# Key sums on VectorE: the second half of a key block is subtracted one step later, and the sums of the batch before are turned and read ahead of the key block

## The chip, the cores and the metric

One core of a Trainium2 chip runs the whole program in one launch. The metric is the device time of the program in microseconds (us), median over several runs; lower is better.

## What is computed

The reference is a small decoder layer stack over x (8 batches of 56 tokens, 256 wide) and a context of 8 batches of 1500 tokens: softmax cross attention, a mixture of experts, a linear cross attention, a second mixture of experts, each with a residual. The change touches only what the linear cross attention takes from the context:

```python
# linear cross attention (L1), per batch and head (16 heads of 16, 64 features)
k = (ctx @ Wk.T + bk)                      # 1500 x 256
v = (ctx @ Wv.T + bv)                      # 1500 x 256
k_prime = relu(einsum('bhnd,fd->bhnf', k, Wkf)) * mask
kv    = einsum('bhnf,bhne->bhfe', k_prime, v)   # 64 x 16 per head
k_sum = sum(k_prime, axis=2)                    # 64 per head
```

All matrix products keep about float32 accuracy: each operand x is held as a rounded part (hi, type fp32r) and a rest (lo = x - hi), and a product is three matmuls: lo by hi, hi by lo, hi by hi (`mm3`, L102 to L106).

## The kernel before

The program has two stages. The first, `sums_and_queries` (L109), computes kv and k_sum of all eight batches, and beside it the normalised queries of the softmax attention. It ends in a barrier of all engines, then `attention_and_after` runs the rest. The change is in the first stage alone.

**Steps.** A batch of 1500 context tokens is 12 steps t of 125 tokens (`KT`), and 3 chunks of 500 (`KC`), 4 steps to a chunk. `step(i, first, last)` is written once for each engine and holds all 12 steps of batch i; `run_peeled` (L217) runs batch 0 by itself (`first`), batches 1 to 6 in a hardware loop, and batch 7 by itself (`last`). Engines meet only through semaphores, and each works through its own list in order.

**A step on TensorE** (L372): `values(i, t)` (6 matmuls into one of two PSUM banks `vals_ps`), `features(i, t)` (8 matmuls in two halves of 4, L282), at every third step `add`, which accumulates vs by kp of three earlier steps into `sums` (L296), then what `keys_at` gives for this step, then the turn of the batch before at t == 4, and for two heads of queries a batch `project` (t = 4 and 8) and `mean_square` (t = 6 and 10, L344).

**Key blocks.** `keys_at` (L208) gives, outside the last batch, one key block at t = 0, 2, 4, 6, 8 and 10: block (c, m) is 500 tokens of chunk c by 128 of the 256 key columns, one chunk ahead of the steps that use it. `keys` on TensorE (L264) makes it in the single bank `keys_ps`, 6 matmuls, after a wait until VectorE has taken both halves of the block before (`ks_lo`, L266). Then come two halves h of 64 partitions each: ScalarE writes the rounded part plus bias (L421, `ks_hi`), VectorE writes the rest (L537, `ks_lo`), which reads `keys_ps`, the bias and ScalarE's result in partitions 0 to 63, and writes partitions 64 to 127 of `ks`. In the last batch the blocks are at t = 0, 2, 3 and 5.

**VectorE's step** (L599): L605 takes values out of PSUM into vs (after `v_done`), L609 takes the second half of the features into kp with relu (after `feat_done`, gives `kp_high`); ScalarE takes the first half (L474, gives `kp_low`). Each half of `feat` is a single bank, so each half of `features(i, t + 1)` waits for `kp_low` or `kp_high` of step t (L288):

```python
for half in range(2):
    wait(pe, ks_lo, 4 * (i * KC + c) + 2 * (half + 1))
    wait(pe, (kp_low, kp_high)[half], i * KT + t)
```

Behind L609 VectorE runs both halves of a key block (L611), at t == 4 `read_blocks` of the batch before (L541), then `round_square` of a query head (L559, at t = 5 and 9) and `normalise` (L565, at t = 7 and 11). `round_square` feeds `split_square` on POOL (L687), and that `mean_square` on TensorE one step later.

**Turn and read.** At t == 3 ScalarE copies the finished sums of the batch before to SBUF (`take_sums`, four L428, `kv_taken`). At t == 4 TensorE transposes them (`turn`, L315, two transposes into the second half of the `sums` bank pair, L319), and VectorE reads the result in six instructions (L548, L550, L554, `kv_done`). `add(i, 0)`, at t == 5, waits for `kv_done` (L304), since it starts `sums` anew.

Of the kernel before, what the change touches and what calls it, by code (L numbers as in the profile page):

```python
# [60 lines left out]
def wait(eng, sem, value):  # L61

    if isinstance(value, int) and value <= 0:
        return
    eng.wait_ge(sem, value)
# [43 lines left out]
def sums_and_queries(nc, kv, qT, q0, raw, ct, kk, wk0, wv0, a, ident):  # L109
# [9 lines left out]
    with ExitStack() as ctx:  # L119
# [84 lines left out]
        def queries_at(i, last, t, after):  # L204

            return [(n, 2 * i + n) for n in range(2) if t - after == ((0, 3) if last else (4, 8))[n]]

        def keys_at(i, last, t):  # L208

            c, n = divmod(t, TPC)  # L210
            if last:
                return {0: [(i, 1, 0)], 2: [(i, 1, 1)], 3: [(i, 2, 0)], 5: [(i, 2, 1)]}.get(t, [])
            if n not in (0, 2):
                return []
            return [(i, c + 1, n // 2)] if c + 1 < KC else [(i + 1, 0, n // 2)]
# [47 lines left out]
        def _(pe):  # L263
# [9 lines left out]
            def values(i, t):  # L273
                c, n = divmod(t, TPC)
                y = slice(n * KP, (n + 1) * KP)
                wait(pe, v_set, i * KT + t - 1)
                for k in range(DC):
                    last = mm3(nc, vals_ps[0:KP, t % 2, 0:D], ct[0][:, c, k, y], ct[1][:, c, k, y],
                               wv[0][:, k, :], wv[1][:, k, :], k == 0, k == DC - 1)
                last.then_inc(v_done, 1)  # L280
# [15 lines left out]
            def add(i, g):  # L296

                n = i * KT + (g + 1) * GROUP
                wait(pe, v_set, n)
                wait(pe, v_mask, n)  # L300
                wait(pe, kp_low, n)
                wait(pe, kp_high, n)
                if g == 0:
                    wait(pe, kv_done, 4 * i)  # L304
                for t in range(g * GROUP, (g + 1) * GROUP):
                    for r in range(4):
                        for j in range(4):
                            h = 8 * (r // 2) + 2 * j + r % 2
                            last = nc.tensor.matmul(sums[32 * j:32 * j + RV, 0, r * FD:(r + 1) * FD],
                                                    vs[:, t % RING, h, :], kp[:, t % RING, h * FD:(h + 1) * FD],  # L310
                                                    start=(t == 0 and r == 0), stop=(t == KT - 1 and r == 3),
                                                    skip_group_check=True)
                last.then_inc(sums_done, 1)

            def turn(i):  # L315

                wait(pe, kv_taken, 4 * (i + 1))
                for n in range(2):
                    last = nc.tensor.transpose(sums[:, 1, n * 128:(n + 1) * 128], sums_sb[:, n * 128:(n + 1) * 128],  # L319
                                               ident[:])  # L320
                last.then_inc(kv_turned, 1)
# [50 lines left out]
            def step(i, first, last):  # L372
                for t in range(KT):
                    values(i, t)
                    features(i, t)
                    if t % GROUP == GROUP - 1:
                        if t >= GROUP:
                            add(i, t // GROUP - 1)
                        elif not first:
                            add(i - 1, NG - 1)  # L380
                    for which in keys_at(i, last, t):
                        keys(*which)
                    if t == 4 and not first:
                        turn(i - 1)
                    if last and t > FIRST_KEYS_AT:
                        key_mean(t - FIRST_KEYS_AT - 1)
                    if last and t >= FIRST_KEYS_AT:
                        key_project(t - FIRST_KEYS_AT)
                    for k, h in queries_at(i, last, t, MEAN_AT):
                        mean_square(h, k)  # L390
                    for k, h in queries_at(i, last, t, 0):
                        project(h, k, i)
# [136 lines left out]

        @block.vector  # L530
        def _(dve):
            def keys(i, c, m):

                for h in range(2):
                    y = slice(64 * h, 64 * (h + 1))
                    wait(dve, ks_hi, 4 * (i * KC + c) + 2 * m + h + 1)
                    nc.vector.scalar_tensor_tensor(ks[64:128, c, 2 * m + h, :], keys_ps[y, 0:CH],  # L537
                                                   bk[y, m:m + 1], ks[0:64, c, 2 * m + h, :].bitcast(F32),
                                                   ALU.add, ALU.subtract).then_inc(ks_lo, 1)

            def read_blocks(i):  # L541

                wait(dve, kv_turned, i + 1)
                src = sums[:, 1, :].rearrange("p (h n) -> p h n", n=32)
                to = kv[:, one(context(i))].rearrange("p a h n -> p (a h) n")
                for n in range(2):
                    r = slice(64 * n, 64 * (n + 1))
                    nc.vector.tensor_tensor(tmp[r], bv[r, :, n, :], src[r, :, HE:RV].to_broadcast([64, NP, HE]),  # L548
                                            ALU.mult).then_inc(tmp_done, 1)
                    nc.vector.tensor_copy(to[r, :, HE], src[r, :, HE]).then_inc(kv_done, 1)  # L550
                for n in range(2):
                    r = slice(64 * n, 64 * (n + 1))
                    wait(dve, tmp_done, 2 * i + n + 1)
                    nc.vector.tensor_tensor(to[r, :, 0:HE], tmp[r], src[r, :, 0:HE], ALU.add).then_inc(kv_done, 1)  # L554
# [44 lines left out]
            def step(i, first, last):  # L599
                for t in range(KT):  # L600
                    m = i * KT + t
                    if t % GROUP == 0:
                        wait(dve, sums_done, NG * i + t // GROUP - 1)
                    wait(dve, v_done, m + 1)
                    nc.vector.tensor_scalar(vs[:, t % RING, :, 0:HE],  # L605
                                            vals_ps[0:KP, t % 2, 0:D].rearrange("p (h e) -> p h e", e=HE),
                                            masks[:, one(context(i) * KT + t), 0], None, ALU.mult).then_inc(v_set, 1)
                    wait(dve, feat_done, 2 * m + 2)
                    nc.vector.tensor_scalar(kp[:, t % RING, 512:1024], feat[0:KP, 1, :], 0.0, None,  # L609
                                            ALU.max).then_inc(kp_high, 1)  # L610
                    for which in keys_at(i, last, t):  # L611
                        keys(*which)
                    if t == 4 and not first:
                        read_blocks(i - 1)
                    if last and t > FIRST_KEYS_AT:
                        key_normalise(t - FIRST_KEYS_AT - 1)
                    if last and t in (7, 8):
                        split_first_queries(t - 7)
                    for k, h in queries_at(i, last, t, SQUARE_AT):
                        round_square(h, k)  # L620
                    for k, h in queries_at(i, last, t, ROOT_AT[last]):
                        normalise(h, k)
                    if first and t == 5:
                        dve.wait_ge(nw_loaded, 32)
                        nc.vector.scalar_tensor_tensor(nw[:, 2:3], nw[:, 0:1], HD ** -0.5, nw[:, 1:2],
                                                       ALU.mult, ALU.mult).then_inc(nw_done, 1)
                        dve.wait_ge(nw_done, 1)
# [27 lines left out]
                                    ALU.subtract).then_inc(f_split, 1)  # L655
            dve.wait_ge(const_loaded, 32)
            dve.wait_ge(set0, 5)
            keys(0, 0, 0)
            for c in range(DC):
                dve.wait_ge(x_hi, c + 1)  # L660
                nc.vector.tensor_tensor(xnT[1][:, c, :], (proj, mean)[c][:, 0:NTOK], xnT[0][:, c, :].bitcast(F32),
                                        ALU.subtract).then_inc((proj_free, mean_free)[c], 1)
            keys(0, 0, 1)
            dve.wait_ge(m_loaded, 16)
            run_peeled(dve, step)
            key_normalise(NK - 1)
# [90 lines left out]
class Norm:  # L757
# [81 lines left out]
    def turn(self, pe, h):  # L839

        pe.wait_ge(self.xn_done, 2 * h + 2)
        for c in range(DC):
            for i in range(2):
                y = c * HT + i * TP
                last = self.nc.tensor.transpose(self.bank[:, 6, y:y + TP],
                                                self.scratch[:, 2 * h + i, c * 128:(c + 1) * 128], self.ident[0:TP, 0:TP])
        last.then_inc(self.turned_done, 1)
# [1627 lines left out]
```

## Time and profile before

| | |
|---|---|
| median of three runs | 1281.7 us (1280.79 to 1281.98) |
| the profiled execution | 1282.82 us |
| its span, first to last instruction | 1281.0 us, so 1.8 us lie around it |
| TensorE busy in the span | 1186.6 us (93%) |
| VectorE, ScalarE, POOL busy | 876.8, 737.7, 536.0 us |
| mean granted TensorE clock | 0.982 of full speed |

Engines in the profile: PE is TensorE's matmuls, PEld its weight loads (one before each matmul), DVE is VectorE, ACT ScalarE, POOL GpSimd, SP SyncE. L12 is line 12 of the kernel. A row of the timeline has start and length in us, engine, line, operation, the tile written and the tiles read, shapes, the count of instructions merged into the row, and in brackets the idle time before it with what ended it. The first stage fills the span up to about 372 us; its loop batches repeat each other to within some hundredths of a microsecond.

### The profile page before, as it was taken

The page shows a single profiled execution, that of the slowest core. Times are in us where ns is not written, and L with a number is a line of the kernel's source. Part 1 is how long each engine was busy: PE and PEld are TensorE (multiplying, and loading weights), DVE is VectorE, ACT ScalarE, POOL GpSimd, SP SyncE. Part 2 cuts the span into 40 slices and gives each one's busy share as a digit, 9 for nine tenths or more (in the row PEclk, how much of TensorE's full clock was granted, in tenths as well). Part 3 has the DMA queues.
Part 4 walks back from the last instruction along what each step waited for, and adds up shares of the span by engine and source line. Part 5 has one row for each costly group of instructions (what it writes and reads, how often), then busy time and mean ns, then how long its engine had stood idle before and what let it go on. Part 6 is the DMA issues. An engine that isn't in the chain of part 4 may idle for free.

```text
span 1281.0 us, 28260 instructions
## 1 busy us (share of the span) xinstructions
PE 1186.6 (93%) x10014; PEld 1055.1 (82%) x10014; DVE 876.8 (68%) x1950; ACT 737.7 (58%) x1330; POOL 536.0 (42%) x561
## 2 busy tenths in 40 slices
PE   5999999999877999999999999999999996898988
PEld 4888888888756878888888788887888896887888
DVE  5656665666556887878878887878787653656664
ACT  4655655655545656667576666665666643545432
POOL 2423232323135365363553544636536674633400
PEclk9999999999988999999999999999999998999999
DMA  4211111110013101111011110110001025014000
GB/s 142 75 43 41 56 32 40 56 40 1 2 40 106 49 25 35 39 48 48 1 47 48 45 51 0 48 48 20 28 0 50 18 75 161 2 52 123 1 8 9
DMA packets 42689, 56.12 MB, mean 44 GB/s; under 512 B 3410, under 2 KB 41602, under 8 KB 42626
## 3 DMA queue, kind: packets, MB, share of 16 engines
q1 hardware_dynamic: 41810, 54.23, 13.4%
q10 hardware_dynamic: 816, 1.05, 0.3%
q8 instruction: 40, 0.66, 0.2%
q14 instruction: 23, 0.19, 0.0%
HBM read 54.81 MB, written 0.46 MB: 43 GB/s over the span
## 4 chain that ended last, share of the span: by engine, by line
PE 57%; DVE 7%; DMA 2%; issue 2%; ACT 2%; SPq 1%; POOL 1%; DVEq 0%; ACTq 0%
PE att_bank L104 16%; PE att_bank L106 14%; PE att_bank L105 14%; PE att_bank L1854 6%; PE att_bank L1812 3%; DMA att_raw_n<-in_ctx 1%; DVE att_cn L2109 1%; DVE att_pr L2163 1%; DMA tail_x<-in_x 1%; SPq L1290 1%; DVE tail_full L1428 1%; PE att_bank L1566 1%; DVE tail_hid L1447 0%; PE att_bank L939 0%; PE att_bank L1384 0%
## 5 line engine op out<-in xcount | busy, mean ns | idle before, releaser
L2335 POOL TENSOR_TENSOR att_sq<-att_work,att_sq 128x500 fp32r<-128x500 f32 x90 | 119.8, 1331 | 160.1 <-DVE att_sq L2129 160.1
L2339 POOL TENSOR_TENSOR attention_kk<-att_work,attention_kk 128x500 fp32r<-128x500 f32 x90 | 121.9, 1354 | 154.1 <-DVE attention_kk L2137 154.1
L104 PE MATMUL att_bank<-att_pT,att_cn 125*128 125x448 f32 x384 | 157.0, 409 | 7.3 <-DVE att_pT L2178 6.6
L1992 ACT ACTIVATE att_pr<-att_pr,att_nmx 112x1500 f32<-112x1500 f32 (+1 forms) x96 | 108.5, 1130 | 71.0 <-DVE att_nmx L2166 71.0
L106 PE MATMUL att_bank<-att_pT,att_cn 125*128 125x448 f32 x384 | 140.9, 367 | 0.0
L105 PE MATMUL att_bank<-att_pT,att_cn 125*128 125x448 f32 x384 | 140.4, 366 | 0.0
L537 DVE SCALAR_TENSOR_TENSOR attention_kk<-kvs_keys_ps,kvs_bk,attention_kk 64x500 fp32r<-64x500 f32 x96 | 70.9, 738 | 92.0 <-ACT attention_kk L421 90.4
L2178 DVE TENSOR_TENSOR att_pT<-att_bank,att_pT 125x448 fp32r<-125x448 f32 x192 | 118.3, 617 | 14.6 <-ACT att_pT L2008 14.3
L2163 DVE TENSOR_SCALAR_CACHE_REDUCE att_pr<-att_bank 112x500 f32<-112x500 f32 x192 | 121.7, 675 | 5.9 <-PE att_bank L106 4.5
L292 PE MATMUL kvs_feat<-kvs_f,attention_kk 128*125 128x256 f32 x768 | 113.0, 284 | 10.8 <-DVE kvs_kp L609 10.1
L1854 PEld LDWEIGHTS att_bank<-all_ident,att_pr 112*125 112x125 f32 x768 | 109.6, 189 | 14.4 <-ACT att_pr L1992 2.3
L421 ACT ACTIVATE attention_kk<-kvs_keys_ps,kvs_bk 64x500 fp32r<-64x500 f32 x96 | 64.7, 674 | 92.6 <-PE kvs_keys_ps L106 91.3
L1854 PE MATMUL att_bank<-all_ident,att_pr 112*125 112x112 f32 x768 | 111.2, 271 | 1.7 <-ACT att_pr L1992 1.7
L292 PEld LDWEIGHTS kvs_feat<-kvs_f,attention_kk 128*125 128x125 f32 x768 | 98.6, 186 | 15.9 <-issue 14.1
L1981 ACT ACTIVATE att_work<-att_bank,att_eps 128x500 f32<-128x500 f32 x90 | 60.7, 674 | 86.8 <-PE att_bank L106 86.8
L2008 ACT ACTIVATE att_pT<-att_bank 125x448 fp32r<-125x448 f32 x192 | 102.2, 532 | 11.4 <-PE att_bank L1854 11.4
L2132 DVE TENSOR_TENSOR att_work<-att_bank,att_work 128x500 f32<-128x500 f32 x90 | 60.9, 677 | 56.4 <-ACT att_work L1988 55.8
L104 PE MATMUL att_bank<-attention_kk,attention_q 128*112 128x500 f32 x192 | 77.4, 403 | 16.6 <-DVE att_pr L2163 11.3
L474 ACT ACTIVATE kvs_kp<-kvs_feat,kvs_zero 125x512 f32<-125x512 f32 x96 | 65.8, 686 | 43.1 <-PE kvs_feat L292 42.6
L1986 ACT ACTIVATE att_work<-att_bank,att_eps 128x500 f32<-128x500 f32 x90 | 61.0, 677 | 48.2 <-PE att_bank L1812 48.2
L104 PEld LDWEIGHTS att_bank<-att_pT,att_cn 125*128 125x128 f32 x384 | 73.2, 191 | 17.5 <-DVE att_pT L2178 11.7
L2129 DVE CAST att_sq<-att_work 128x500 fp32r<-128x500 f32 x90 | 51.4, 571 | 40.1 <-ACT att_work L1981 40.1
(279 smaller groups left out, 3416.9 us busy)
## 6 DMA issues: line engine op xcount, KB each, us to landing
attention_raw_t<-in_ctxT SPq DMA_DIRECT2D x45, 500.0 KB, 4.0
att_raw_n<-in_ctx SPq DMA_DIRECT2D x16, 750.0 KB
kvs_raw_q<-in_wq SPq DMA_DIRECT2D x8, 256.0 KB, 3.9
tail_wo_raw<-in_wo SPq DMA_DIRECT2D x4, 512.0 KB, 4.4
tail_down_w<-in_down SPq DMA_DIRECT2D x8, 256.0 KB, 3.8
tail_gate_w<-in_gate SPq DMA_DIRECT2D x7, 256.0 KB, 2.8
tail_up_w<-in_up SPq DMA_DIRECT2D x7, 256.0 KB, 3.1
tail_gate_w<-in_gate SPq DMA_DIRECT2D x1, 1760.0 KB, 7.0
```

What stands on the lines that cost most here:

```text
L104: nc.tensor.matmul(out, w_lo, x_hi, start=start, stop=False, skip_group_check=True)
L105: nc.tensor.matmul(out, w_hi, x_lo, start=False, stop=False, skip_group_check=True)
L106: return nc.tensor.matmul(out, w_hi, x_hi, start=False, stop=stop, skip_group_check=True)
L292: last = nc.tensor.matmul(feat[0:KP, half, z], ks[:, c, 2 * half + g, y], f2[:, w, :], start=(w == 1), stop=(w == 0), skip_group_check=True)
L537: nc.vector.scalar_tensor_tensor(ks[64:128, c, 2 * m + h, :], keys_ps[y, 0:CH], bk[y, m:m + 1], ks[0:64, c, 2 * m + h, :].bitcast(F32), AL ...
L1854: last = nc.tensor.transpose(ring[0:KP, t % 3, j * TP:(j + 1) * TP], pr[:, j, t * KP:(t + 1) * KP], ident[0:TP, 0:TP])
L1992: nc.scalar.activation(pr[:, j, keys], pr[:, j, keys], ACT.Exp, scale=-1.0, bias=nmx[:, j:j + 1], accum_out=z[:, 4 * u + j, c:c + 1]).then ...
L2008: nc.scalar.activation(pT[0][:, t % 3, :], ring[0:KP, t % 3, 0:QU], ACT.Copy).then_inc(pT_hi, 1)
L2163: nc.vector.tensor_scalar(pr[:, j, c * CH:(c + 1) * CH], ring[0:TP, c, 0:CH], -1.0, 3.0e38, ALU.mult, ALU.min, accum_out=mn[:, j, c:c + 1] ...
L2178: nc.vector.tensor_tensor(pT[1][:, t % 3, :], ring[0:KP, t % 3, 0:QU], pT[0][:, t % 3, :].bitcast(F32), ALU.subtract).then_inc(ring_free, 1)
L2335: nc.gpsimd.tensor_tensor(sq[1][:, i % 2, :], work[:, i % 2, :], sq[0][:, i % 2, :].bitcast(F32), ALU.subtract).then_inc(sq_lo, 1)
L2339: nc.gpsimd.tensor_tensor(kk[:, c, 2 + gi, :], work[:, i % 2, :], kk[:, c, gi, :].bitcast(F32), ALU.subtract).then_inc(k_lo, 1)
```

## The change

TensorE does the turn of the batch before ahead of the key block of t == 4 and no longer behind it. VectorE reads the turned sums ahead of that block. Outside the last batch VectorE subtracts only the first half of a key block in the block's own step; the second half comes in the next step, behind that step's L605 and L609 and ahead of `round_square` and `normalise`. Blocks are only at even t up to 10, so none is left over at a batch's end. The last batch and the two blocks ahead of batch 0 keep both halves together. No instruction is added or taken away, on any engine or DMA queue.

```diff
@@ TensorE, step
+                    if t == 4 and not first:
+                        turn(i - 1)
                     for which in keys_at(i, last, t):
                         keys(*which)
-                    if t == 4 and not first:
-                        turn(i - 1)
@@ VectorE
-            def keys(i, c, m):
-
-                for h in range(2):
+            def keys(i, c, m, halves):
+
+                for h in halves:
                     y = slice(64 * h, 64 * (h + 1))
                     wait(dve, ks_hi, 4 * (i * KC + c) + 2 * m + h + 1)
@@ VectorE, step
                     wait(dve, feat_done, 2 * m + 2)
                     nc.vector.tensor_scalar(kp[:, t % RING, 512:1024], feat[0:KP, 1, :], 0.0, None,
                                             ALU.max).then_inc(kp_high, 1)
-                    for which in keys_at(i, last, t):
-                        keys(*which)
                     if t == 4 and not first:
                         read_blocks(i - 1)
+                    if not last and t > 0:
+                        for which in keys_at(i, last, t - 1):
+                            keys(*which, (1,))
+                    for which in keys_at(i, last, t):
+                        keys(*which, (0, 1) if last else (0,))
@@ VectorE, ahead of batch 0
-            keys(0, 0, 0)
+            keys(0, 0, 0, (0, 1))
...
-            keys(0, 0, 1)
+            keys(0, 0, 1, (0, 1))
```

## Rows read from the trace of the kernel before

**Rows 1.** Busy time by stretch, us; then granted clock, DMA share, GB/s
```profile
core 0: us, PE busy (x) PEld busy (x) DVE busy (x) ACT busy (x) POOL busy (x), PEclk, DMA share, GB/s
102.00:144.00 42.00, 39.60 (x648) 36.16 (x638) 25.77 (x48) 24.46 (x40) 12.73 (x18) 1.00 0.15 43
...
372.00:392.00 20.00, 14.69 (x60) 11.12 (x60) 10.62 (x41) 10.92 (x18) 5.82 (x12) 0.84 0.53 141
```

**Rows 2.** Waits of PE, 30 to 370 us: total, times, longest
```profile
PE kvs_feat L292 <- DVE kvs_kp L609: 9.6, 20, 0.6
PE kvs_sums L309 <- DVE all_kv L554: 5.6, 7, 0.8
```

**Rows 3.** Timeline of weight loads, a loop batch, t = 4 to project
```profile
115.77 0.53 PEld L292 LDWEIGHTS kvs_feat<-kvs_f,attention_kk 128*125 128x125 f32 x4
117.08 0.54 PEld L292 LDWEIGHTS kvs_feat<-kvs_f,attention_kk 128*125 128x125 f32 x4 [0.77 <-issue]
117.55 0.19 PEld L104 LDWEIGHTS kvs_keys_ps<-attention_ct,kvs_wk 128*128 128x128 f32 x1
...
118.79 0.36 PEld L319 LDWEIGHTS kvs_sums<-all_ident,kvs_sums_sb 128*128 128x128 f32 x2
119.12 0.19 PEld L104 LDWEIGHTS kvs_proj<-kvs_xnT,kvs_wq 128*128 128x128 f32 x1
```

**Rows 4.** Timeline of VectorE, the same loop batch, t = 2 to 5
```profile
114.34 1.51 DVE L537 SCALAR_TENSOR_TENSOR attention_kk<-kvs_keys_ps,kvs_bk,attention_kk 64x500 fp32r<-64x500 f32 x2 [3.05 <-ACT attention_kk L421]
115.88 0.48 DVE L605 TENSOR_SCALAR kvs_vs<-kvs_vals_ps,kvs_masks 125x256 f32<-125x256 f32 x1
116.28 0.68 DVE L609 TENSOR_SCALAR kvs_kp<-kvs_feat 125x512 f32<-125x512 f32 x1
116.88 0.48 DVE L605 TENSOR_SCALAR kvs_vs<-kvs_vals_ps,kvs_masks 125x256 f32<-125x256 f32 x1
...
121.54 0.28 DVE L548 TENSOR_TENSOR kvs_tmp<-kvs_bv,kvs_sums 64x128 f32<-64x128 f32 x1
121.75 0.16 DVE L550 COPY all_kv<-kvs_sums 64x8 f32 x1
121.94 0.29 DVE L548 TENSOR_TENSOR kvs_tmp<-kvs_bv,kvs_sums 64x128 f32<-64x128 f32 x1
...
122.98 0.48 DVE L605 TENSOR_SCALAR kvs_vs<-kvs_vals_ps,kvs_masks 125x256 f32<-125x256 f32 x1
```

**Rows 5.** Timeline of weight loads: batch 0, then t = 5, 8 and 11
```profile
29.50 0.53 PEld L292 LDWEIGHTS kvs_feat<-kvs_f,attention_kk 128*125 128x125 f32 x4 [0.71 <-issue]
...
121.05 1.01 PEld L292 LDWEIGHTS kvs_feat<-kvs_f,attention_kk 128*125 128x125 f32 x8
...
123.07 1.39 PEld L309 LDWEIGHTS kvs_sums<-kvs_kp,kvs_vs 125*17 125x17 f32 x96 [1.00 <-issue]
...
130.32 0.54 PEld L292 LDWEIGHTS kvs_feat<-kvs_f,attention_kk 128*125 128x125 f32 x4
131.31 0.53 PEld L292 LDWEIGHTS kvs_feat<-kvs_f,attention_kk 128*125 128x125 f32 x4 [0.45 <-issue]
...
141.81 1.02 PEld L292 LDWEIGHTS kvs_feat<-kvs_f,attention_kk 128*125 128x125 f32 x8
142.97 1.36 PEld L309 LDWEIGHTS kvs_sums<-kvs_kp,kvs_vs 125*17 125x17 f32 x96
```

**Rows 6.** Timeline of ScalarE at t = 3: the four copies of take_sums
```profile
115.61 1.55 ACT L428 ACTIVATE kvs_sums_sb<-kvs_sums 17x256 f32<-17x256 f32 x4
```

**Rows 7.** Timeline of VectorE at t = 9
```profile
138.00 0.69 DVE L609 TENSOR_SCALAR kvs_kp<-kvs_feat 125x512 f32<-125x512 f32 x1 [0.16 <-PE kvs_feat L292]
138.76 0.39 DVE L559 CAST kvs_sq<-kvs_work 128x448 fp32r<-128x448 f32 x1
```

**Rows 8.** Timeline of POOL, t = 9
```profile
139.24 1.16 POOL L687 TENSOR_TENSOR kvs_sq<-kvs_work,kvs_sq 128x448 fp32r<-128x448 f32 x1 [5.29 <-DVE kvs_sq L559]
```

**Rows 9.** Timeline of weight loads, t = 10: key block and mean square
```profile
139.34 0.19 PEld L104 LDWEIGHTS kvs_keys_ps<-attention_ct,kvs_wk 128*128 128x128 f32 x1
...
140.59 0.41 PEld L349 LDWEIGHTS kvs_mean<-kvs_sq,kvs_mean_mat 128*128 128x128 f32 x2
```

## The prediction

> **What bounds the kernel now.** I read the busy times by stretch first. In a loop batch of the first stage TensorE's matmuls are busy for 39.60 of 42 us while VectorE has 25.77, ScalarE 24.46 and POOL 12.73, and the clock is granted in full [rows 1]. So TensorE sets the pace, and the stage gets shorter only by what TensorE stands still. Next I read who TensorE waits for in this stage. Two waits carry nearly all of it: the second half of the features waits for VectorE's L609, 20 times, and the sums wait for the read of the turned sums, 7 times [rows 2]. The change aims at these two. The stage ends in a barrier of all engines and the next one starts its own loads behind it, so I count a microsecond saved here as a microsecond of the total.
>
> The totals of the waits are too small, since a matmul's modelled end reaches into the gap, so I take sizes from the weight loads. At t = 4 the two halves of the features start at 115.77 and 117.08, and an unhindered half takes 117.55 - 117.08 = 0.47. The second could have started at 116.24: TensorE loses 0.84 [rows 3]. The cause is in VectorE's rows: two L537 of the key block from 114.34, L605 at 115.88, L609 at 116.28 to 116.96, and TensorE starts 0.12 after that end, which I use below as the lag from any engine to TensorE [rows 3, 4]. The same happens at t = 2 (no row shown, same sizes). At t = 8 the loss is 131.31 - (130.32 + 0.47) = 0.52 [rows 5]. At t = 5 the add starts at 123.07, where its features started at 121.05; undisturbed it comes 142.97 - 141.81 = 1.16 after them, so 0.86 is lost [rows 5]. Key blocks at t = 4, 8 and 10 lose nothing to their own second half: an add, a project or a mean square lies between the block and the features in question.
>
> **Part 1: the second half one step later.** One L537 with its gap is 0.77 (two take 115.88 - 114.34 = 1.54) [rows 4]. L605 and L609 of the step behind the block come 0.77 sooner: at t = 3, L609 at 115.51, done 116.19, TensorE served at 116.31. Against 116.24 that leaves 0.07, so **0.77 is gained at t = 4 and the same at t = 2**. At t = 8, 0.77 covers the whole 0.52: **0.52 gained**.
>
> What becomes late instead? The deferred L537 starts behind L609. How soon, the trace doesn't show for this pair, so I bound it: 0.60 after L609's start if it overlaps like the L605 at 116.88, or 0.03 after L609's end, 0.71, if it behaves like instructions that change their partition half [rows 4]. The two L548 and the L550 between them decide for me: L550, in the same half as the L548 ahead, starts 0.21 after that 0.28 long one, before it ends; the second L548, in the other half, starts 0.19 after a 0.16 long L550, behind its end [rows 4]. L537 writes the upper half, L609 the lower, so I take 0.71. The Trainium skill says the same against this change in "VectorE: DVE Perf Modes", section "Two Vector instructions with no wait between them": an instruction whose start quadrant differs from the last one's starts only when all earlier ones are done. By that rule the sum below stands, and the trace agrees as far as these rows go. With 0.60 instead of 0.71, the key block of t = 10 in seven batches and the two waits in batch 0 below would each be 0.11 shorter, a gain of 1 us more.
>
> So at t = 3 the deferred L537 runs 116.22 to 116.96 and TensorE knows at 117.08. Three waits hang on it:
> - The next key block needs `keys_ps` back. At t = 2 and 8 of a loop batch an add comes first, at t = 6 and 0 too (one step before): nothing; at t = 4 the turn (part 2) waits longer anyway. In batch 0 there is no add at t = 2 and no turn: the block can start at 29.50, where the stalled half starts now, and not 29.97; instead of 0.77 **0.47 is gained, twice** [rows 3, 5].
> - At t = 10 no add comes between. L609 of t = 9 starts at 138.00 because TensorE's features end there, so it doesn't move sooner. The deferred L537 runs 138.71 to 139.45, TensorE may start the block at 139.57 and not 139.34: **0.23 lost** [rows 7, 9].
> - L559 stands behind it: 139.48 for 138.76, 0.72 later. POOL's split follows, 139.96 for 139.24, done 141.12, and the mean square is served at 141.24. It would have been due at 140.59 + 0.23 = 140.82: **0.42 lost** [rows 7, 8, 9]. At t = 5 the same delay has more than 3 us before the mean square of t = 6, and I cost it at nothing. L565 at t = 7 and 11 waits for ScalarE anyway.
>
> **Part 2: turn and read first.** The turn needs ScalarE's four copies, done at 117.16 [rows 6]. That was covered by the key block. Now TensorE is through with the features at 116.31 + 0.47 = 116.78 and waits until 117.28. The turn costs the same 119.12 - 118.79 = 0.33 as before, the key block 118.79 - 117.55 = 1.24, so the project starts at 118.85 for 119.12. Of the 0.77 won at t = 4 **only 0.27 is left** [rows 3, 6]. If the lag from ScalarE is nothing, 0.39 is left.
> In return the read, 122.98 - 121.54 = 1.44 long, starts behind L609 of t = 4 at about 118.0 and ends by 119.5, where VectorE now stands idle waiting for ScalarE's half of the block, and `kv_done` is there well over 2 us before the add: **0.86 gained** [rows 4, 5]. If something unseen holds VectorE in that gap, the price is that the read goes behind again, and the 0.86 stays lost.
>
> **The sum.** Loop batch: 0.77 + 0.27 + 0.86 + 0.52 - 0.23 - 0.42 = 1.77, six times 10.6. Batch 0: 0.47 + 0.47 + 0.52 - 0.65 = 0.8. Batch 7: both halves stay together and no block stands at t = 4: 0. Together 11.4 us. From the profiled execution's 1282.8 that gives 1271.4; the median lies 1.1 lower, so 1270.3. The lags are rather rounded up, so I say **1270.0**.
>
> **Rivals.**
> - *A, both new waits stay away.* If the split is in time at t = 10 and the copies at t = 4, a loop batch gains 0.77 + 0.77 + 0.86 + 0.52 = 2.92 and batch 0 gains 2.06: 19.6 us, 1262.1. For it: the new waits are sums of several small lags. Against: the 0.50 at the turn follows from one row, and ScalarE's order isn't touched. If only the t = 10 losses stay away, it is 16 us, 1265.7. Chance of the two 0.18.
> - *B, the half isn't what TensorE waits for.* If `kp_low` of ScalarE were as late as `kp_high`, L609 would be served earlier for nothing: six times 0.86 is left, less seven times 0.65: 0.6 us, 1281.1. Against: the first half of the features, served by ScalarE, starts 1.31 before the second [rows 3]. Chance 0.03.
> - *C, slower: the deferred half holds up every block.* The mechanism is that of t = 10: the L537 now waits in line for an L609 that itself waits for TensorE, then TensorE waits for the L537 and for the square's split. If the 0.65 arose at all six blocks of seven batches, 27 us, less the 19.6 gained, the time would be 1289. It decides from a loss of 0.47 a block. Against: an add, the turn or a project stands ahead of or behind the other blocks, and only two blocks have a square behind them. Chance 0.02.
> - *D, the clock.* The lower level, 1.2 for 2.4 GHz, showed as 0.84 granted behind the barrier, where TensorE had stood still [rows 1]. The change makes the stage denser, and there the clock was full. A low stretch of 24 us would eat the gain and leave about 1281.7. Chance 0.02.
>
> **How the numbers follow.** My forecast has 0.75, with 8 to 15 us gained from the bounds above (stalls that come back in part, lags of 0 to 0.12). The range takes in the lesser form of A and ends ahead of B: 1264.5 to 1274.5. A measurement of this kernel can tell 0.2%, 2.6 us, from no change. Faster has the forecast and A, 0.93; within 0.2% B and D, 0.05; slower C, 0.02.
>
> **What would show it.** In a loop batch the 0.77 and 0.45 idle ahead of L292 (t = 2, 4, 8) and the 1.00 ahead of L309 (t = 5) should be gone; L319 should stand ahead of the key block with about 0.5 idle ended by ScalarE's L428; a short idle ahead of the key block of t = 10, and one of about 0.4 ahead of L349, ended by POOL. The batch's period should fall by 1.8 us, and the second stage keep its length. I am wrong if the period falls by under 1.2 or over 2.4, or if the second stage changes by over 2 us.

## The result and the profile after

The changed kernel takes 1274.87 us (median of five, 1273.24 to 1277.79) against 1281.83 us before (five runs beside it); the ratio is 0.9947, 95% interval 0.9933 to 0.9961. It is faster, by 7.0 us, where 11.7 were forecast, and 0.4 us beyond the range's upper end. The profiled execution took 1277.79 us, span 1276.0 us.

The gain came from where it was looked for, but not all of it. The second stage's first matmul starts at 366.47 us in the profile after, and at 373.29 before: the first stage is 6.8 us shorter, nearly the whole gain of the medians. The stretch of a loop batch, the same columns as in [rows 1]:

```profile
102.00:144.00 42.00, 41.04 (x621) 37.36 (x620) 26.65 (x48) 24.68 (x40) 14.03 (x20) 1.00 0.17 53
```

TensorE is busy for 41.04 of 42 us and not 39.60. What it still waits for between 20 and 370 us (total, times, longest), against [rows 2], whose window begins 10 us later:

```profile
PE kvs_feat L292 <- DVE attention_kk L537: 6.2, 15, 0.5
...
PE kvs_sums L309 <- DVE all_kv L554: 0.6, 1, 0.6
```

The wait for the read of the sums is gone but for the last batch. The features no longer wait for L609. They wait for **L537**, the very instruction that was moved, 15 times: twice in each of the seven batches outside the last, and once at the first step of batch 0. That last one isn't new. The kernel before has it too, at a time that the window of [rows 2] leaves out:

```profile
23.91 0.54 PEld L292 LDWEIGHTS kvs_feat<-kvs_f,attention_kk 128*125 128x125 f32 x4 [0.85 <-DVE attention_kk L537]
```

The weight loads say where; this is the loop batch that answers to [rows 3, 5, 9]:

```profile
113.67 0.53 PEld L292 LDWEIGHTS kvs_feat<-kvs_f,attention_kk 128*125 128x125 f32 x4
114.91 0.53 PEld L292 LDWEIGHTS kvs_feat<-kvs_f,attention_kk 128*125 128x125 f32 x4 [0.71 <-DVE attention_kk L537]
115.39 0.25 PEld L319 LDWEIGHTS kvs_sums<-all_ident,kvs_sums_sb 128*128 128x128 f32 x2
115.61 0.19 PEld L104 LDWEIGHTS kvs_keys_ps<-attention_ct,kvs_wk 128*128 128x128 f32 x1
...
118.87 1.02 PEld L292 LDWEIGHTS kvs_feat<-kvs_f,attention_kk 128*125 128x125 f32 x8
120.03 1.36 PEld L309 LDWEIGHTS kvs_sums<-kvs_kp,kvs_vs 125*17 125x17 f32 x96
...
127.27 0.54 PEld L292 LDWEIGHTS kvs_feat<-kvs_f,attention_kk 128*125 128x125 f32 x4
128.40 0.53 PEld L292 LDWEIGHTS kvs_feat<-kvs_f,attention_kk 128*125 128x125 f32 x4 [0.59 <-DVE attention_kk L537]
...
135.48 1.01 PEld L292 LDWEIGHTS kvs_feat<-kvs_f,attention_kk 128*125 128x125 f32 x8
136.61 0.19 PEld L104 LDWEIGHTS kvs_keys_ps<-attention_ct,kvs_wk 128*128 128x128 f32 x1
...
138.26 0.30 PEld L349 LDWEIGHTS kvs_mean<-kvs_sq,kvs_mean_mat 128*128 128x128 f32 x2 [0.44 <-POOL kvs_sq L690]
```

At t = 4 the second half of the features starts 114.91 - 113.67 = 1.24 after the first, where 0.47 is its own pace: 0.77 is lost, for 0.84 before. At t = 8 it is 128.40 - 127.27 - 0.47 = 0.66, for 0.52 before: more, not less. The add of t = 5 comes 1.16 after its features, undisturbed. At t = 10 the key block stands 1.13 behind the start of its features instead of the 0.94 or 0.95 of eight loads, and the mean square waits for POOL. At t = 2 no row has an idle time: that stall is gone.

VectorE's rows for t = 2 to 4, against [rows 4]:

```profile
112.24 0.73 DVE L537 SCALAR_TENSOR_TENSOR attention_kk<-kvs_keys_ps,kvs_bk,attention_kk 64x500 fp32r<-64x500 f32 x1 [2.73 <-ACT attention_kk L421]
113.00 0.48 DVE L605 TENSOR_SCALAR kvs_vs<-kvs_vals_ps,kvs_masks 125x256 f32<-125x256 f32 x1
113.40 0.68 DVE L609 TENSOR_SCALAR kvs_kp<-kvs_feat 125x512 f32<-125x512 f32 x1
114.11 0.75 DVE L537 SCALAR_TENSOR_TENSOR attention_kk<-kvs_keys_ps,kvs_bk,attention_kk 64x500 fp32r<-64x500 f32 x1
...
116.31 0.27 DVE L548 TENSOR_TENSOR kvs_tmp<-kvs_bv,kvs_sums 64x128 f32<-64x128 f32 x1
...
118.05 0.73 DVE L537 SCALAR_TENSOR_TENSOR attention_kk<-kvs_keys_ps,kvs_bk,attention_kk 64x500 fp32r<-64x500 f32 x1 [0.35 <-ACT attention_kk L421]
```

L609 did come sooner: done at 114.08, in time for TensorE's half, which was due at 113.67 + 0.47 = 114.14. The deferred L537 starts at 114.11, ends at 114.86, and TensorE goes on at 114.91. The code says why. Step 4 is the first step of chunk 1, and the second half of `features` waits at L287 for all four halves of that chunk's keys. The last of them is the second half of the block of t = 2: the half that was moved. The same holds for t = 8 and the block of t = 6. The deferral took L537 from ahead of L609 and put it behind, while both are wanted at the same instant.

My theory after reading this: of the deferral only the block of t = 0 pays; those of t = 2 and 6 bring nothing, that of t = 8 costs at t = 10. The rival is the prediction's account, in which t = 4 and 8 profit too. In all of what follows "batch" is the distance between the same load in two loop batches that follow each other: 41.60 us before (the stall of t = 2 stands at 109.82 and 151.41, which is 41.59), 155.34 - 114.91 = 40.43 after. Over the five distances from the stall of t = 4 in batch 1 to that in batch 6 the means are 41.61 and 40.47, and in every kernel below such a mean lies within 0.05 of the one distance given. So differences of a few hundredths between batches mean nothing.

### The profile page after: what moved, and what is told of

It is laid out like the page before. It is cut to its first block, busy times and chain, and to the rows that moved or that the text cites. A ratio compares the mean times of both kernels' runs of the same rounds, so it can differ in the third digit from the quotient of the medians.

```text
span 1276.0 us, 28260 instructions
## 1 busy us (share of the span) xinstructions
PE 1190.6 (93%) x10014; PEld 1056.9 (83%) x10014; DVE 879.2 (69%) x1950; ACT 738.2 (58%) x1330; POOL 536.0 (42%) x561
## 4 chain that ended last, share of the span: by engine, by line
PE 57%; DVE 7%; DMA 2%; issue 2%; ACT 2%; SPq 1%; POOL 1%; DVEq 0%; ACTq 0%
PE att_bank L104 16%; PE att_bank L106 14%; PE att_bank L105 14%; PE att_bank L1857 6%; PE att_bank L1815 3%; DMA att_raw_n<-in_ctx 1%; DVE att_cn L2112 1%; DVE att_pr L2166 1%; DMA tail_x<-in_x 1%; SPq L1293 1%; DVE tail_full L1431 1%; PE att_bank L1569 1%; DVE tail_hid L1450 0%; PE att_bank L942 0%; PE att_bank L1387 0%
## 5 line engine op out<-in xcount | busy, mean ns | idle before, releaser
L537 DVE SCALAR_TENSOR_TENSOR attention_kk<-kvs_keys_ps,kvs_bk,attention_kk 64x500 fp32r<-64x500 f32 x96 | 70.9, 738 | 81.5 <-ACT attention_kk L421 79.9
L104 PEld LDWEIGHTS att_bank<-att_pT,att_cn 125*128 125x128 f32 x384 | 73.2, 191 | 17.4 <-DVE att_pT L2181 11.7
```

The source lines that it names most:

```text
L104: nc.tensor.matmul(out, w_lo, x_hi, start=start, stop=False, skip_group_check=True)
```

## The experiments

### The turn and read alone

```diff
 # on the kernel before: the two moves around turn() and read_blocks(), and no deferral
+                    if t == 4 and not first:
+                        read_blocks(i - 1)
                     for which in keys_at(i, last, t):
                         keys(*which)
-                    if t == 4 and not first:
-                        read_blocks(i - 1)
```

> Only the turn and the read of the last batch's sums go ahead of the key block; both halves of a key block stay together. Theory (each stall of TensorE belongs to one named wait, and they add up): the 1.00 idle ahead of L309 at t = 5 goes, worth 0.86, and the turn costs 0.22 ahead of the block instead of 0.33 behind it; the stalls at t = 2, 4 and 8 (0.84, 0.84, 0.52) stay. A loop batch falls from 41.60 to about 40.65 us, the first stage by 5.7 us, the time to about 1276. Rival (the read was only late because the whole key block was): the read now ends earlier but the add still stands behind something else, and the batch stays above 41.2.

Measured: 1276.38 us, ratio 0.9952 (0.9935 to 0.9969). Weight loads of one loop batch, and the first stall of the next:

```profile
108.77 0.52 PEld L292 LDWEIGHTS kvs_feat<-kvs_f,attention_kk 128*125 128x125 f32 x4 [0.78 <-issue]
115.99 0.53 PEld L292 LDWEIGHTS kvs_feat<-kvs_f,attention_kk 128*125 128x125 f32 x4 [0.77 <-issue]
129.34 0.53 PEld L292 LDWEIGHTS kvs_feat<-kvs_f,attention_kk 128*125 128x125 f32 x4 [0.45 <-issue]
...
149.44 0.53 PEld L292 LDWEIGHTS kvs_feat<-kvs_f,attention_kk 128*125 128x125 f32 x4 [0.79 <-issue]
```

The three stalls of the features stand as before, the one of the add is gone, and the batch is 40.67 us. This part alone brings 0.93 a batch, most of what the whole change brings.

### The deferral alone

```diff
 # on the changed kernel: TensorE's turn behind the key block again, and VectorE's read behind it
-                    if t == 4 and not first:
-                        read_blocks(i - 1)
                     if not last and t > 0:
...
                         keys(*which, (0, 1) if last else (0,))
+                    if t == 4 and not first:
+                        read_blocks(i - 1)
```

> Only the second half of a key block is deferred; the turn stays behind the key block and the read behind the block's first half. Theory (the features of a chunk's first step need that chunk's own second key block complete, L287): 0.77 gained at t = 2, 0.07 at t = 4 and 0.14 lost at t = 8, both then waiting for L537, about 0.54 lost at t = 10; the read of t = 4 starts one L537 sooner, so that the add of t = 5 loses almost nothing: 0.8 gained. Batch about 40.65 us, time about 1276. Rival (the recorded prediction: deferral gives 0.77, 0.77 and 0.52 and loses 0.65): 1.4 from these plus the 0.8 of the read, batch 39.4 us.

Measured: 1276.57 us, ratio 0.9957 (0.9941 to 0.9974).

```profile
115.42 0.53 PEld L292 LDWEIGHTS kvs_feat<-kvs_f,attention_kk 128*125 128x125 f32 x4 [0.72 <-DVE attention_kk L537]
120.63 1.39 PEld L309 LDWEIGHTS kvs_sums<-kvs_kp,kvs_vs 125*17 125x17 f32 x96 [0.23 <-issue]
129.03 0.53 PEld L292 LDWEIGHTS kvs_feat<-kvs_f,attention_kk 128*125 128x125 f32 x4 [0.59 <-DVE attention_kk L537]
...
156.04 0.53 PEld L292 LDWEIGHTS kvs_feat<-kvs_f,attention_kk 128*125 128x125 f32 x4 [0.71 <-DVE attention_kk L537]
```

The batch is 40.62 us, where the rival wanted 39.4, and both stalls are ended by L537. The two parts are not independent: with one L537 fewer ahead of the read, the add's idle time falls from 1.00 to 0.23 although the turn wasn't moved. So the parts alone bring 0.93 and 0.98, and both at once 1.17 and not 1.91: the stall of the add is counted in both.

### Deferring the block of t = 0 only

```diff
-                    if not last and t > 0:
+                    if not last and t - 1 in (0,):
...
-                        keys(*which, (0, 1) if last else (0,))
+                        keys(*which, (0,) if not last and t in (0,) else (0, 1))
```

> Turn and read ahead as in the changed kernel, but only the block of t = 0 is deferred; those of t = 2, 4, 6, 8 and 10 keep both halves together. Theory: 0.77 at t = 2, 0.86 at t = 5, 0.11 at the turn, nothing lost at t = 8 and 10, the stall of t = 4 as before (0.84, ended by L609): batch 39.9 us, 0.6 below the changed kernel's 40.44; time about 1271 with the second stage as it was. Rival (what the other deferred halves give outweighs what they cost): the batch is longer than the changed kernel's 40.44.

Measured: 1272.28 us, ratio 0.992 (0.9903 to 0.9937).

```profile
113.64 0.53 PEld L292 LDWEIGHTS kvs_feat<-kvs_f,attention_kk 128*125 128x125 f32 x4 [0.78 <-issue]
126.98 0.54 PEld L292 LDWEIGHTS kvs_feat<-kvs_f,attention_kk 128*125 128x125 f32 x4 [0.45 <-issue]
...
153.59 0.53 PEld L292 LDWEIGHTS kvs_feat<-kvs_f,attention_kk 128*125 128x125 f32 x4 [0.78 <-issue]
```

Batch 39.95 us. Taking five of the six deferrals back makes a loop batch 0.48 shorter than the changed kernel's. Against the turn and read alone, the deferral of t = 0 is worth 40.67 - 39.95 = 0.72.

### Deferring the first blocks of the chunks, and the second blocks

These two are each other's complement: the same two lines, with `(0, 4, 8)` in the first kernel and `(2, 6, 10)` in the second.

> As e3, but the blocks of t = 0, 4 and 8 are deferred (the first blocks of their chunks, which no features need in the next two steps). Theory: as e3, plus the loss at t = 10 (key block and mean square wait for the deferred half of t = 8), about 0.54: batch 40.4 us; the stall of t = 8 is 0.52 again, ended by L609 and not by L537. Rival (the loss at t = 10 comes from the block of t = 6 or 10 being deferred): batch 39.9 us as e3.

> The opposite of e4: turn and read ahead, only the blocks of t = 2, 6 and 10 deferred, the second blocks of their chunks. Theory: they bring nothing, since the features two steps later need both their halves: 0.84 stays at t = 2, t = 4 gains 0.07, t = 8 loses 0.14, both ended by L537, nothing lost at t = 10; with 0.86 of the add and 0.11 of the turn the batch is 40.7 us, as long as with the turn and read alone (40.67). Rival (recorded prediction): t = 4 and 8 gain up to 0.77 and 0.52 less the wait at the turn, batch 39.7 us.

Measured: 1275.09 us, ratio 0.9951 (0.9934 to 0.9968), and 1276.29 us, ratio 0.9962 (0.9947 to 0.9977). Weight loads, with t = 0, 4 and 8 deferred:

```profile
115.23 0.53 PEld L292 LDWEIGHTS kvs_feat<-kvs_f,attention_kk 128*125 128x125 f32 x4 [0.78 <-issue]
128.60 0.54 PEld L292 LDWEIGHTS kvs_feat<-kvs_f,attention_kk 128*125 128x125 f32 x4 [0.45 <-issue]
...
138.49 0.30 PEld L349 LDWEIGHTS kvs_mean<-kvs_sq,kvs_mean_mat 128*128 128x128 f32 x2 [0.45 <-POOL kvs_sq L690]
...
155.66 0.53 PEld L292 LDWEIGHTS kvs_feat<-kvs_f,attention_kk 128*125 128x125 f32 x4 [0.78 <-issue]
```

and with t = 2, 6 and 10 deferred:

```profile
108.94 0.53 PEld L292 LDWEIGHTS kvs_feat<-kvs_f,attention_kk 128*125 128x125 f32 x4 [0.79 <-issue]
116.14 0.53 PEld L292 LDWEIGHTS kvs_feat<-kvs_f,attention_kk 128*125 128x125 f32 x4 [0.71 <-DVE attention_kk L537]
129.64 0.53 PEld L292 LDWEIGHTS kvs_feat<-kvs_f,attention_kk 128*125 128x125 f32 x4 [0.59 <-DVE attention_kk L537]
...
156.91 0.53 PEld L292 LDWEIGHTS kvs_feat<-kvs_f,attention_kk 128*125 128x125 f32 x4 [0.71 <-DVE attention_kk L537]
```

The stall that L537 ends is there exactly when the second blocks are deferred, and then the mean square isn't late; with the first blocks it is the other way round. Batches: 40.43, so the half of t = 8 (with that of t = 4, which meets no wait in the profile after) costs 0.48 against deferring t = 0 alone; and 40.77, so the halves of t = 2, 6 and 10 bring nothing and cost 0.10 against the turn and read alone. That settles the cause. The blocks of t = 4 and t = 10 were deferred only together with others, so neither has a price of its own.

### The square ahead of the deferred half

```diff
 # on the changed kernel
+                    for k, h in queries_at(i, last, t, SQUARE_AT):
+                        round_square(h, k)
                     if not last and t > 0:
...
-                    for k, h in queries_at(i, last, t, SQUARE_AT):
-                        round_square(h, k)
```

> The changed kernel with the deferred half behind round_square (L559) instead of ahead of it. Theory: the square's split is in time and the 0.45 idle ahead of the mean square of t = 10 goes, but the key block of t = 10 waits as much longer (0.19 becomes about 0.65), since L559 waits for ScalarE and the half stands behind it: batch 40.4 to 40.5 us, no gain. Rival (the two losses at t = 10 are independent of the order): the 0.45 goes and the key block waits 0.2 as before, batch 40.0 us.

One run, 1276.41 us, so the time has no interval; the reading rests on the trace.

```profile
137.40 0.19 PEld L104 LDWEIGHTS kvs_keys_ps<-attention_ct,kvs_wk 128*128 128x128 f32 x1 [0.58 <-DVE attention_kk L537]
...
138.66 0.41 PEld L349 LDWEIGHTS kvs_mean<-kvs_sq,kvs_mean_mat 128*128 128x128 f32 x2
```

The mean square waits no longer, and the key block of t = 10 has 0.58 idle ahead of it, as the theory had it. But the batch is 40.71 us (155.93 - 115.22), 0.2 to 0.3 above what I gave. Most of that is that the 0.44 idle ahead of the mean square in the changed kernel is not all lost time. Its load comes 138.26 - 136.61 = 1.65 behind the key block there and 138.66 - 137.40 = 1.26 here, so it is 0.39 late; and behind it the loads take 3.84 us to the next batch's first there and 3.98 here, so 0.14 is made up again. The two losses of t = 10 are thus 0.19 + 0.39 - 0.14 = 0.44 in the changed kernel. The rest, under 0.1, I did not trace.

### L609 ahead of L605 in steps 3 and 7

If both halves and L609 are wanted together at t = 4 and 8, the thing to take out of their way is L605, whose result TensorE wants only two steps on.

```diff
 # on the kernel that defers t = 0 only; part 0 is L605 with its wait, part 1 is L609 with its wait
+                    for part in ((1, 0) if not last and t in (3, 7) else (0, 1)):
```

> As e3, and in steps 3 and 7 VectorE does L609 ahead of L605, so that the feature half TensorE waits for comes 0.40 sooner while both halves of the key block stay in their own step. Theory: the stall of t = 4 falls from 0.84 to 0.44, that of t = 8 from 0.52 to 0.12: batch 39.95 - 0.80 = 39.15 us, first stage 4.8 + 0.8 = 5.6 us below e3, time about 1267. Rival (L605 put behind makes the values of a later step wait): the batch stays at 39.9 and TensorE shows waits for L605.

Measured: **1266.36 us, ratio 0.988 (0.9865 to 0.9895)**, faster than both kernels. VectorE at t = 2 to 4 (L613 is L609 of the other kernels, L607 is L605), then the loads of TensorE:

```profile
109.43 1.51 DVE L537 SCALAR_TENSOR_TENSOR attention_kk<-kvs_keys_ps,kvs_bk,attention_kk 64x500 fp32r<-64x500 f32 x2 [2.72 <-ACT attention_kk L421]
110.97 0.69 DVE L613 TENSOR_SCALAR kvs_kp<-kvs_feat 125x512 f32<-125x512 f32 x1
111.58 0.87 DVE L607 TENSOR_SCALAR kvs_vs<-kvs_vals_ps,kvs_masks 125x256 f32<-125x256 f32 x2
```

```profile
111.78 0.53 PEld L292 LDWEIGHTS kvs_feat<-kvs_f,attention_kk 128*125 128x125 f32 x4 [0.39 <-issue]
...
150.95 0.53 PEld L292 LDWEIGHTS kvs_feat<-kvs_f,attention_kk 128*125 128x125 f32 x4 [0.39 <-issue]
```

The batch is 39.17 us, 0.78 less for 0.80 expected. The stall of t = 4 is halved, that of t = 8 too small to be listed, and nothing waits for L607. The first stage is 4.9 us shorter than with t = 0 deferred only (357.41 against 362.33), a little less than the 5.6 expected; six times 0.78 is 4.7.

### The changed kernel once more

> The changed kernel once more, unaltered, for a second profile of it. Theory (the first stage repeats to a tenth of a microsecond and the scatter lies in the second stage, with TensorE's granted clock): the second stage's first matmul at 366.5 again, and the rest of the span between 905 and 910 us, longer when the mean clock is lower. Rival (the change lengthens the second stage by 1.8 us every time): 909.5 again, and the time 1277.

Measured: 1275.19 us, ratio 0.9941 (0.9928 to 0.9955). The batch is 40.46 us (155.27 - 114.81), and the second stage begins at 365.89, not at 366.5: 0.6 sooner. Almost all of it arises in one place of the last batch: the last weight load of the add at t = 5 stands behind an idle time of 1.92 us and not 2.46 (327.46 for 328.04), though the load ahead of it starts within 0.04 in both. The profile names nothing that it waits for. So the theory holds for the loop and not for the end of the stage, and the lengths of the first stage of two kernels can be compared only to about half a microsecond; the idle time at this place is 1.91 to 2.46 in nine of the ten profiles and 0.62 with t = 2, 6 and 10 deferred. The batch is the better measure.

The rest of the span is 1274.8 - 365.89 = 908.9 us. That lies in the theory's 905 to 910 and close to the rival's 909.5, so this run doesn't part the two, the more so as both profiles of the changed kernel are of the slowest of its five runs (1277.79 and 1276.66).

## Why the prediction was wrong

The direction and the bound were right; the sum for a loop batch was 1.5 times too large. Term by term, us in a loop batch:

| term | predicted | measured |
|---|---|---|
| t = 2, deferral | +0.77 | +0.72 (t = 0 deferred against turn and read alone) |
| t = 4, deferral | +0.77 | +0.07 (0.84 to 0.77 lost) |
| turn ahead of the block | -0.50 | no wait; the load of the turn takes 0.22 for 0.33 |
| t = 5, read ahead | +0.86 | with the turn, +0.93 |
| t = 8, deferral | +0.52 | -0.14 (0.52 to 0.66 lost) |
| t = 10, key block and mean square | -0.65 | -0.48 |
| whole batch | +1.77 (sum) | +1.17 (41.60 to 40.43) |

The measured terms add up to 1.10 and not to 1.17, since they come from different kernels and each is good to some hundredths. The period fell by a little less than the 1.2 under which the prediction calls itself wrong.

**The step that failed** is in part 1: "0.77 is gained at t = 4 and the same at t = 2", with "0.77 covers the whole 0.52" at t = 8. I priced L609 coming sooner as if `kp_high` were all that the second half of the features waits for. The quoted code has two waits ahead of it, and I followed the deferred half only to its next key block, to TensorE's turn and to the square ("Three waits hang on it"). The fourth wait, L287, asks for something new only at t = 4, 8 and 0, the first steps of the chunks, and there it asks for exactly the instruction moved. What the runs showed in place of the 0.77 and 0.52 is 0.07 gained at t = 4 and 0.14 lost at t = 8, with TensorE released by L537 both times. In the loop batches of the trace of before this wait never shows, since L537 ran ahead of L609: the wait recorded was for the later of the two, L609. It does show once, at 23.91 us, at the first step of batch 0 (0.85 idle, ended by L537), and the window from 30 us in [rows 2] left that out. At t = 0 of a loop batch an add stands between, and nothing was lost.

**The turn's wait** followed the same mistake. Since the features of t = 4 go on at 114.91 and not 0.7 sooner, ScalarE's copies are done by the time the turn comes, and 0.50 of cost never arose. The two errors partly cancel: that without L287 the sum would have come near 1.77 is only argued, since the features can't do without that half.

**What held.** The read at t = 4 fits where VectorE stood idle, at 116.31, and the add's 0.86 is gone. The deferred L537 starts 114.11 - 113.40 = 0.71 behind the start of L609, as taken from the pair of L548. The cited rule of the Trainium skill, in "VectorE: DVE Perf Modes", section "Two Vector instructions with no wait between them", says that such an instruction starts when all earlier ones are done, and the trace agrees: L609 ends at 114.08, L537 starts at 114.11. The key block of t = 10 lost 0.19 for 0.23. The mean square was over-priced at 0.42: its load shows 0.44 idle, but the two losses of t = 10 together are 0.48, measured as the difference between two kernels. The lag of 0.12 taken from L609 "to TensorE" was too long for the others: TensorE's load starts 0.05 behind the end of L537 (114.86 to 114.91). In batch 0 the same holds as in the loop batches: t = 2 gains the 0.47 forecast, t = 4 only 0.09 of its 0.47.

**The rivals.** A, in which both new waits stay away, was wrong in one of them. C named the right engine and instruction, a deferred half holding up TensorE, but at the key blocks and not at the features, and for far too much. B came closer than its 0.03: at t = 4 and 8 L609 is indeed served earlier for nothing, though what TensorE then waits for is L537 and not `kp_low`. D did not show in the first stage.

**The time** then follows: six times 1.17 is 7.0 us, batch 0 brings about nothing (0.56 gained from its first stall to that of t = 4, 35.10 - 23.91 before and 34.28 - 23.65 after, and lost again by t = 11) where 0.8 was forecast, and the first stage is 6.8 us shorter. No case of the range, 8 to 15 us gained, had the deferral bring nothing at t = 4 and 8.

## What to carry to other kernels

Before moving an instruction, list every semaphore that it raises and every wait on that semaphore, above all those that show in the trace nowhere, or only once outside the loop: a wait can be satisfied early just because of the order that you are about to change. Where several results of one engine are wanted at one instant, moving one behind another brings nothing; take out of their way what is wanted later, as L605 here. And where a move is made in six places, price each place by itself: here one of six paid (t = 0), two brought TensorE next to nothing at the features they serve (t = 2 and 6), and one (t = 8) cost about 0.48 us a batch, where the whole change gained 1.17.

## What was not expected of the hardware

The second stage, whose code is the same in all these kernels, is not equally long. From its first matmul to the end of the span it takes 907.7 us before (1281.0 - 373.29), 907.9 with the turn and read alone, 909.5 and 908.9 in the two profiles of the changed kernel, and 906.0 to 910.2 in the others. The longest, 910.2 with t = 0 deferred only, has the lowest mean granted clock of the ten, 0.978, and the shortest, 906.0 with t = 0, 4 and 8 deferred, has the highest, 0.983. In both profiles of the changed kernel one place sticks out. Stretch 1012 to 1020 us (columns as in [rows 1]), before (where the program is 6.8 us less far on at that time), after, after once more, and with t = 0, 4 and 8 deferred:

```profile
1012.00:1020.00 8.00, 6.29 (x30) 4.63 (x28) 7.83 (x26) 5.72 (x8) 7.67 (x6) 1.00 0.00 1
```

```profile
1012.00:1020.00 8.00, 8.00 (x50) 7.70 (x49) 3.77 (x8) 5.27 (x11) 6.35 (x4) 0.79 0.01 2
```

```profile
1012.00:1020.00 8.00, 8.00 (x50) 7.71 (x50) 4.12 (x9) 5.75 (x12) 5.85 (x4) 0.79 0.01 2
```

```profile
1012.00:1020.00 8.00, 8.00 (x61) 7.75 (x60) 5.29 (x12) 6.20 (x12) 6.72 (x4) 1.00 0.01 2
```

The granted clock of these 8 us is 0.79 of the 2.4 GHz level in the changed kernel, a mean that has time at 1.2 GHz in it (from 1014 to 1016 us it is 0.50), behind a stretch in which TensorE stood still (5.29 of 7 us busy between 1005 and 1012 in both). From VectorE's L2146 to its first L1000 the changed kernel needs 1018.37 - 1010.78 = 7.59 us. In the kernel before the same two instructions (L2143, L997) are 5.99 apart, and in the seven other kernels 5.98 or 5.99. So the low stretch costs 1.6 us when it falls there.

Neither the standstill nor the length of the first stage explains it alone. With t = 0, 4 and 8 deferred TensorE is busy for the same 5.29 of 7 us between 1005 and 1012, and the second stage begins at 365.94, between the 365.89 and 366.47 of the two profiles of the changed kernel, yet the clock stays at 1.00. What decides it, and whether the shortest runs of the changed kernel, 1273.1 to 1273.6 us, are those without it, no profile here shows.
